# Queries and keys of an attention pass's first head computed in the preceding pass, and unread matmuls around the second layer norm

## The reference, cut to what matters

```python
x1 = _ln(x) * (1.0 + scale1) + shift1
qkv = (x1 @ qkv_w + qkv_b).reshape(Bc, Tc, 3, H, DH)      # 16 heads of 128
attn = softmax(einsum('bthd,bshd->bhts', q, k) * scale)
attn_out = einsum('bhts,bshd->bthd', attn, v) @ out_w + out_b
x = x + gate1 * attn_out
x2 = _ln(x) * (1.0 + scale2) + shift2
x = x + gate2 * (gelu(x2 @ ffn_w1 + ffn_b1) @ ffn_w2 + ffn_b2)
x = x + _L0_attn_ref(x)                                    # a minimal GRU, two 256x256 gates
x = x + _L0_ffn_ref(_L0_cond2_ref(cond, cond, x, ...))     # 32 steps of RK4, then top 4 of 16 blocks
```

## Time and profile before

| | us |
|---|---|
| median of 3 runs | 516.11 |
| the profiled execution | 515.61 |
| its span, from the first to the last instruction | 513.8 |
| PE busy | 449.6 (88%) |
| DVE busy | 434.9 (85%) |
| ACT busy | 316.3 (62%) |
| POOL busy | 48.6 (9%) |

### The profile page before, as it was taken

One profiled execution on the slowest core, in us unless ns is written; L12 is line 12 of the kernel. 1 busy time (PEld: TensorE's weight loads), 2 busy tenths in 40 slices (PEclk: granted clock), 3 DMA queues, 4 the chain that ended last, 5 costly groups with the idle time before them and its releaser, 6 DMA issues.

```text
span 513.8 us, 13730 instructions
## 1 busy us (share of the span) xinstructions
PE 449.6 (88%) x4980; PEld 307.5 (60%) x4980; DVE 434.9 (85%) x1705; ACT 316.3 (62%) x880; POOL 48.6 (9%) x77
## 2 busy tenths in 40 slices
PE   2999989998999899997498997689888888888887
PEld 2655665567556665575244443667676766766666
DVE  4969786787777876889988786999999999999994
ACT  1387855786487748786458755465655646555563
POOL 3010330224021211123000000000000000000000
PEclk9999999999999999999789999698989999999999
DMA  8972402200202000000000000000000000000000
GB/s 294 417 311 63 106 7 76 61 21 0 82 21 62 0 0 1 0 1 0 0 1 1 0 1 0 3 3 0 1 1 11 11 1 10 1 11 11 1 10 22
DMA packets 10127, 20.82 MB, mean 41 GB/s; under 512 B 1456, under 2 KB 4720, under 8 KB 9456
## 3 DMA queue, kind: packets, MB, share of 16 engines
q1 hardware_dynamic: 9536, 19.89, 11.2%
q10 hardware_dynamic: 560, 0.60, 0.3%
HBM read 19.40 MB, written 1.08 MB: 40 GB/s over the span
## 4 chain that ended last, share of the span: by engine, by line
DVE 42%; PE 40%; ACT 6%; issue 5%; POOL 4%; DMA 1%; ACTq 0%; DVEq 0%
PE bank L804 34%; DVE base L1649 5%; DVE lin L1751 5%; POOL ptx L477 4%; DVE qs L1655 4%; DVE cub L1643 3%; PE score L804 3%; DVE sq L1637 3%; DVE pacc L1761 3%; PE spare L804 2%; ACT ao_sb L541 2%; DVE thlo L1633 1%; DMA vec<-vecs 1%; DVE qn L1655 1%; DVE acc L1421 1%
## 5 line engine op out<-in xcount | busy, mean ns | idle before, releaser
L804 PE MATMUL bank<-x,pairs_store 128*128 128x512 f16 x384 | 85.6, 379 | 0.0
L804 PE MATMUL score<-th,coup_part 128*128 128x32 f16 x1024 | 47.2, 179 | 18.1 <-ACT th L788 17.2
L804 PEld LDWEIGHTS bank<-x,pairs_store 128*128 128x128 f16 x384 | 37.1, 98 | 42.8 <-DVE x L1219 0.4
L477 POOL TENSOR_TENSOR ptx<-pt,ptx 32x256 f16<-32x256 f32 x64 | 44.7, 699 | 189.4 <-ACT ptx L573 185.8
L541 ACT ACTIVATE big<-bank,pass_b 128x512 f16<-128x512 f32 x64 | 42.1, 684 | 24.3 <-DVE pass_b L1347 14.4
L788 ACT ACTIVATE th<-qs 128x64 f16<-128x64 f32 x96 | 24.5, 255 | 47.5 <-DVE qs L1655 47.5
L804 PEld LDWEIGHTS score<-th,coup_part 128*128 128x128 f16 x1024 | 34.7, 97 | 31.1 <-ACT th L788 29.7
L1359 DVE SCALAR_TENSOR_TENSOR big<-bank,pass_b,big 128x512 f16<-128x512 f32 x64 | 45.7, 742 | 8.0 <-ACT big L541 7.3
L804 PE MATMUL bank<-pairs_store,ao_sb 128*128 128x256 f16 x384 | 46.6, 273 | 4.7 <-DVE acc L1421 1.4
L804 PEld LDWEIGHTS bank<-pairs_store,ao_sb 128*128 128x128 f16 x384 | 35.5, 97 | 13.6 <-issue 3.6
L804 PE MATMUL bank<-pairs_store,x 128*128 128x512 f16 x192 | 43.4, 379 | 0.0
(11 more groups left out here) (210 smaller groups left out, 1041.8 us busy)
## 6 DMA issues: line engine op xcount, KB each, us to landing
wqk_sb<-wqk SPq DMA_DIRECT2D x16, 256.0 KB, 3.0
wv_sb<-wv SPq DMA_DIRECT2D x4, 512.0 KB, 5.6
wo_sb<-wo SPq DMA_DIRECT2D x4, 512.0 KB, 4.2
f_sb<-ffn_w SPq DMA_DIRECT2D x2, 1024.0 KB, 14.2
ao_sb<-xtok SPq DMA_DIRECT2D x4, 256.0 KB, 6.1
big<-ada_w SPq DMA_DIRECT2D x1, 1024.0 KB, 9.7
x_sb<-xT SPq DMA_DIRECT2D x1, 1024.0 KB, 13.3
w_sb<-w1T SPq DMA_DIRECT2D x1, 1024.0 KB, 16.4
```

What stands on the lines that cost most here:

```text
L477: nc.gpsimd.tensor_tensor(ptx[s, 1, :, s], pt[s], ptx[s, 0, :, s], ALU.subtract).then_inc(ptx_ready, 1)
L804: return nc.tensor.matmul(dst, lhsT, rhs, start=start, stop=stop, **kw)
```

## The change

It moves the queries and keys of a pass's first head to the preceding pass. Those of pass 0 are made ahead of the passes. In passes 0 to 2 `project_next(0, 1)` stands on PE ahead of `mix(2)` and `project_next(2, 3)` ahead of the last two out projections; ACT and DVE have their parts of it at matching places, and the next pass's weights are split there too, with the first head's weights ahead of the fourth emptying of `project(3)`. PE's passes are a loop of three and a last one written out. The numbers of the bank uses are dealt anew. In passes 0 to 2 ACT copies all four strips of the last head's scores, and DVE's order behind them is another; in the last pass DVE's order stays as it was, without the first head. ACT's roundings for the later feed-forward layer (`mlp_highs`) in the last pass are spread: four of the first five stand at values that ACT empties, and the fifth behind three emptyings of `project(3)`. DVE's places for their low parts are the same. The biases of all heads are scaled once, not in each pass.

Then 41 matmuls of 512 columns whose results nobody reads are added: 6 between `turn_x2(0)` and `turn_normed(0)`, 15 behind `turn_normed(0)`, 20 behind `last_gates()`.

```diff
-USE_PROJ = [0, 10, 16, 22]
-USE_V = [4, 5, 6, 7, 8, 9, 14, 15]
-USE_PV = [20, 26, 30, 35]
-USE_OUT = [[28, 29, 32, 37], [33, 34, 38, 39]]
+USE_V = [0, 1, 2, 3, 4, 5, 10, 11]
+USE_PROJ = [[26, 27, 38, 39], [6, 7, 8, 9], [12, 13, 14, 15], [18, 19, 20, 21]]
+USE_PV = [16, 22, 28, 33]
+USE_OUT = [[24, 25, 30, 35], [31, 32, 36, 37]]
...
@@ ScalarE, one pass
+                last = i == NQUAD - 1
+                empty_values(0)
+                if last:
+                    mlp_highs(0, 1)
                 empty_values(1)
...
                 copy_scores(2)
                 empty_projs(3, (0, 1, 2))
+                if last:
+                    mlp_highs(4, 5)
+                else:
+                    weights_high(i + 1, 0)
+                empty_projs(3, [3])
                 exps(2)
-                empty_projs(3, [3])
                 empty_pv(1)
-                copy_scores(3, NB4 // 2)
+                copy_scores(3, NB4 // 2 if last else NB4)
                 place_high(2)
                 exps(3)
+                if not last:
+                    empty_next_proj(0, 1)
                 empty_pv(2)
                 place_high(3)
...
@@ TensorE, one pass
+                def project_next(*ks):
+
+                    if last:
+                        return
+                    if ks[0] == 0:
+                        pe.wait_ge(split_ready, i * NSPLIT + NSPLIT + 1)
+                    for k in ks:
+                        projection(USE_PROJ[0][k], 0, k, fill(USE_PROJ[0][k]))
...
                 def scores(j):
                     if j:
                         pe.wait_ge(scores_copied, i * (QUAD * NB4) + NB4 * j)
+                    else:
+                        for use in USE_V[1:5]:
+                            fill(use)
...
-                project(0)
                 values(0, 1)
                 scores(0)
...
                 out_project(0, 1, [0, 1])
+                project_next(0, 1)
                 mix(2)
...
                 out_project(1, 1, [3])
+                project_next(2, 3)
                 out_project(1, 2, [2, 3])
                 out_project(1, 3, [2, 3])
...
@@ TensorE, behind the passes
+            def unread(dst, count):
+
+                for _ in range(count):
+                    mm(dst, scaled_eye[:], ptx[:, 0, 0:G // 2].rearrange("p g n -> p (g n)"), True, True)
+
+            pe.wait_ge(eye_ready, 1)
             turn_x2(0)
+            unread(spare[:], 6)
             turn_normed(0)
+            unread(spare[:], 15)
...
             last_gates()
+            unread(score[:, 1], 20)
...
@@ VectorE, one pass
-                low_projs(0)
                 low_values(0, 1)
...
-                low_projs(3)
+                last = i == NQUAD - 1
+                for k in range(4):
+                    if k == 3 and not last:
+                        low_weights(i + 1, 0)
+                    low_proj(3, k)
                 low_pv(1, [0])
                 normalise(2)
...
+                else:
+                    low_pv(1, [1])
+                    shift(3)
+                    add_heads(0, 0)
+                    add_heads(0, 1)
+                    normalise(3)
+                    low_first_head(0, (i + 1) * QUAD)
+                    low_first_head(1, (i + 1) * QUAD)
+                    low_pv(2)
+                    add_heads(0, 2)
+                    low_weights(i + 1, 1, 2, 3)
                     low_pv(3)
+                    add_heads(0, 3)
+                    add_heads(1, 0)
+                    add_heads(1, 1)
+                    low_first_head(2, (i + 1) * QUAD)
+                    low_first_head(3, (i + 1) * QUAD)
+                    add_heads(1, 2)
+                    add_heads(1, 3)
```

More of the change, by code:

```diff
@@ L360, in bank_of, with count_of @@
             return use % NBANK
-        def count_of(use, start=0):
-            return start * (USES_PER_PASS // NBANK) + use // NBANK + 1
+        def count_of(use, last=False):
+            if use >= AFTER:
+                return use // NBANK + 1
+            missing = last and use > USE_PROJ[0][1] and bank_of(use) in (1, 2)
+            return FIRST_USES[bank_of(use)] - missing + use // NBANK + 1
         NPAR = USES_PER_PASS // NBANK
@@ L532, in _ @@
             act.wait_ge(ptx_cleared, 1)
+            act.wait_ge(bias_ready, 3)
+            for k, use in enumerate(USE_PROJ[0]):
+                h, w = k // 2, k % 2
+                act.wait_ge(full[bank_of(use)], 1)
+                nc.scalar.activation(qk_sb[:, 0, w, 0, h * HALF:(h + 1) * HALF], bank[bank_of(use)][:], ACT.Identity,
+                                     bias=head_b[:, w, 0:1]).then_inc(high_ready, 1)
             for i in range(NQUAD):
                 def high(use, dst, bias=None):
-                    act.wait_ge(full[bank_of(use)], i * NPAR + count_of(use))
+                    act.wait_ge(full[bank_of(use)], i * NPAR + count_of(use, i == NQUAD - 1))
                     src = bank[bank_of(use)][:]
@@ L581, in empty_values @@
                         high(USE_V[g], v_sb[:, g, 0])
[L583 to L595, removed]
+                last = i == NQUAD - 1
+                empty_values(0)
+                if last:
+                    mlp_highs(0, 1)
                 empty_values(1)
+                if last:
+                    mlp_highs(1, 2)
                 copy_scores(0)
@@ L603, in _ @@
                 empty_values(5)
+                if last:
+                    mlp_highs(3, 4)
                 empty_projs(1, (0, 1))
@@ L840, in _, with projection, attention_pass @@
             ada_chunks(spare[:, D:], 3 * KB, 6 * KB).then_inc(ada2_summed, 1)
-            with pe.Fori(0, NQUAD) as i:
+            def projection(use, j, k, dst):
+                h, w = k // 2, k % 2
+                weights = wqk_pair[:, j % 2].rearrange("p c (k w d) -> p c k w d", k=KB, w=2)
+                sum3(dst[:], [(weights[:, :, n, w], x1_pair[:, :, n, h * HALF:(h + 1) * HALF]) for n in range(KB)]
+                     ).then_inc(full[bank_of(use)], 1)
+            pe.wait_ge(split_ready, 1)
+            for k, use in enumerate(USE_PROJ[0]):
+                pe.wait_ge(x1_ready, k // 2 + 1)
+                pe.wait_ge(free[bank_of(use)], 1)
+                projection(use, 0, k, bank[bank_of(use)])
+            def attention_pass(i, last):
                 def fill(use):
-                    pe.wait_ge(free[bank_of(use)], i * NPAR + count_of(use))
+                    pe.wait_ge(free[bank_of(use)], i * NPAR + count_of(use, last))
                     return bank[bank_of(use)]
                 def taken(use):
-                    pe.wait_ge(free[bank_of(use)], i * NPAR + count_of(use) + 1)
+                    pe.wait_ge(free[bank_of(use)], i * NPAR + count_of(use, last) + 1)
                 def project(j):
                     pe.wait_ge(split_ready, i * NSPLIT + SPLIT_ORDER.index(("qk", j)) + 1)
[L854 to L860, removed]
-                                          for k in range(KB)]).then_inc(full[bank_of(use)], 1)
+                    for k, use in enumerate(USE_PROJ[j]):
+                        projection(use, j, k, fill(use))
+                def project_next(*ks):
+                    if last:
+                        return
+                    if ks[0] == 0:
+                        pe.wait_ge(split_ready, i * NSPLIT + NSPLIT + 1)
+                    for k in ks:
+                        projection(USE_PROJ[0][k], 0, k, fill(USE_PROJ[0][k]))
                 def scores(j):
@@ L1485, in _ @@
                     last_heads(2)
-                assert own.n == STEPS and pairs[0] == PAIRS
+                assert own.n == STEPS and pairs[0] == (i + 1) * PAIRS + (0 if last else 4)
             own.n, own.base = start + NQUAD * STEPS, 0
```

100 lines of the change are left out of this document (60 added, 40 removed).

## The result

| | before | changed |
|---|---|---|
| median, us | 515.95 (515.54 to 516.94, 4 runs) | 523.36 (523.03 to 524.36, 4 runs) |
| ratio | | 1.0144, 95% interval 1.0124 to 1.0164 |
| profiled execution, its span | 515.61, 513.8 | 523.03, 521.3 |

The change makes the kernel 1.4% slower, where 515.2 us was forecast. The forecast's range ended at 517.5.

The account below looks back on a forecast made before the run. PE was taken to pace ordinary passes, DVE the neuron loop. Attention 6.0 - 0.15 - 5.25 = 0.6, taken as 0.8, plus 0.1 for unread matmuls gave 0.9 us off 516.11: 515.2 us, range 512.5 to 517.5.

Parts of the forecast that it names:

- Ordinary passes: Passes 0 to 2: next head's projections fill PE's stops near each pass's end; gain 2.0 us each, 6.0 together.
- Rival 3: Ordinary passes gain only about 1.1 us each, as ACT delays POOL and `mix(3)`; 2.1 lost, 518.2 us; chance 0.13.
- Start of pass 0: In pass 0 `scores(0)` waits for four freed banks at its start, not two; 0.15 us lost once.
- First, the fifth rounding: Last pass: DVE waits for ACT's late fifth rounding of the later layer's weights; everything after is 2.4 us later.
- Rival 1: Last pass loses only one of its two waits, the 2.4 being absorbed; gain 3.3, 512.8 us; chance 0.14.
- Second, the banks: Last pass: `mix(2)` waits for bank 4, emptied late by DVE; both waits together make `mix(3)`'s second part 5.25 us later.
- Everything behind is DVE's chain from 240.14 over the layer norm, unchanged: Behind the last pass's `mix(3)`: DVE sets the pace through the layer norm, and the change adds no loss.
- They delay nothing as long as the clock is full: Second layer norm: the 6 and 15 unread matmuls end before the hidden layer; value zero, bounds -1.8 and +2.16 us.
- rival 2: Clock is on the path: hidden layer's 2.16 us come through, 0.4 at the loop; gain 3.4, 512.7 us; chance 0.07.
- the 0.1 for the 20 ahead of the loop: Behind the gates: 20 unread matmuls may keep the clock up for the neuron loop; 0.1 us gained, bounds 0 and 0.5.
- a last pass more than 6.5 us longer: Sign of a wrong forecast: last pass, first values to last projection, less than 4 or more than 6.5 us longer.
- the page's rule for the clock: Loss is throttled time times one minus clock ratio; some 10 us for two half-clock stretches, not used in the sum.

Follow-up runs that it names:

- e1: Changed kernel with ScalarE making the fifth rounding early, right behind the fourth: 518.91 us, ratio 1.0059 to before.
- e2: Changed kernel with only the bank numbering behind the passes turned by three: 517.83 us, ratio 1.0038 to before.
- e4: Changed kernel with banks numbered without a gap in the last pass and behind it, plus the early fifth rounding: 509.98 us, ratio 0.989 to before.
- e5: Changed kernel without its 41 unread matmuls: 520.61 us, ratio 1.009 to before.
- e7: e4 without the 41 unread matmuls: 510.77 us, ratio 0.9889 to before.
- e9: e1 with 28, 20 and 32 unread matmuls of 128 columns in the last pass's three stops: 517.56 us, ratio 1.0025 to before.
- e3: Changed kernel with banks of the last pass and all behind it numbered without a gap: 512.98 us, ratio 0.9945 to before.
- e6: Kernel before, with the 41 unread matmuls added at the same three places: 515.78 us, ratio 0.9995 to before.
- e8: e4 with 12 and 30 unread matmuls in place of 6 and 15: 510.48 us, ratio 0.9884 to before.

## Why the prediction was wrong

The span was forecast 0.9 us shorter and is 7.5 longer. Of these 8.4 us, 4.8 lie behind the passes, 1.8 in the last pass, 0.9 at the start of pass 0, 0.4 in the ordinary passes, 0.2 behind the start of the output layer, and 0.3 are what the forecast added to its layout.

- **Ordinary passes**, 2.0 us each: the mechanism is right, and they gain 1.9. 54.07 us forecast as 54.0; no stop before `mix(2)`. The stop left before the second part of `mix(3)` is 0.92 us and was put at 0.4, while the wait before `out_project(1, 0, [2])` was put at 0.5 and is 0.2; the two nearly cancel, which is luck. `mix(3)` ends at 181.90, which on the time scale of the kernel before (2.74 us later, by the pass's first values) is 184.64, forecast 184.55. Gain 5.65 in the trace for 6.0 forecast. Rival 3 is out.
- **Start of pass 0**, 0.15 lost: 1.03 in the changed kernel's trace, whose first 24 matmuls take 7.03 us with the clock falling on part of them. In e1, e2, e4, e5, e7 and e9 they run at full clock, `scores(0)` then waits 0.40 us for DVE's emptying, and the first values start at 25.7 to 26.2. The slow clock is not a property of the change; how often it comes no run here shows.
- **"First, the fifth rounding"**, 2.4 us: right. DVE waits 4.61 us for `wv_sb` (4 to 5 were forecast), and it costs 2.3 us between e3 and e4. Rival 1 is out.
- **"Second, the banks"**, 2.85 us: the mechanism and the places are right (waits for `ao_sb`, `acc`, `acc`), the size is not, and the failed step is the full clock at which the layout ran on behind the stops ("PE, waiting for bank 0 until 240.7, then does 24 x 0.110"). Up to there the layout holds: on the time scale of the kernel before (4.62 us later, by the last pass's first values) the changed kernel's second half of `mix(2)` starts at 237.56, forecast 237.75. Around and behind it the granted clock is 0.57 and 0.50 (232 to 236 and 236 to 239 us), and the 16 and the 24 matmuls take 1.89 and 4.09 us, where 1.07 and 2.78 are theirs at full clock: 2.1 us more. In e1 the banks cost 5.1: 2.9 of waits, as forecast, and 2.2 of clock (e9), which the sum left out without a reason. The prediction held a last pass more than 6.5 us longer to show it wrong; it is 7.1 longer.
- **"Everything behind is DVE's chain from 240.14 over the layer norm, unchanged"**: this is the step that failed most, by 4.8 us. The banks were followed to the last pass's `mix(3)` and no further. Output projections (1, 2) and (1, 3) moved from banks 3 and 4 to 1 and 2, while what stands behind the passes kept banks 0, 1, then 2. PE waits for banks that DVE frees only in `last_heads(2)` and `last_heads(3)`, and DVE's way to `last_heads(3)` leads over PE's transposes. e2 shows it: one line on the numbering takes all of it back.
- **"They delay nothing as long as the clock is full"**, said of the unread matmuls, with a bound of -1.8: it holds in the kernel before (e6) and with the banks put right (e4, e7, e8). In the changed kernel the clock was at half and the first 6 stood behind a wait for a bank: 2.5 us (e5), part of the 4.8. The hidden layer's 48 matmuls, forecast at 10.5 us, take 12.15. Speeding them up is worth nothing in e6 and between e7 and e4, so rival 2 is out, and the 0.1 for the 20 ahead of the loop is not to be told from nothing: from the output layer to the end before and e6 take 240.6 and 241.0 us.
- On the page's rule for the clock (the Trainium skill, "TensorE: Matmul & The Clock Gate", section "Terms"): it would give 5 us in the second layer norm before, where a mean of 0.63 over 14 us is 10.4 us at half clock, an estimate by that rule. e6 brings the clock to full there and gains 0.05%, within its interval of zero. In the last pass of e1, where PE is the engine waited for, the clock did cost 2.2 us. The trace disagrees with the rule where another engine holds the path. Where PE does, it bears out the direction: by the rule, 0.66 over 10 us would be 3.4 us in e1, an estimate, and 2.2 were measured.

The range failed because its slow side ended at a last pass that goes as computed. The two large misses have two causes. The waits that a table of banks brings were priced where the diff moved code, and not where the table was merely kept; and those that were priced were priced as waits alone, with the clock at full behind them.

## What to carry to other kernels

When a rotation of buffers is renumbered, follow each buffer past the end of the changed code to its next user, and look at which engine frees it and what that engine waits for in turn; a collision behind the loop cost 4.8 us here and one line removed it. Price a stop of TensorE as the stop and what the clock does behind it, if the matmuls behind it are on the path. Matmuls that hold the clock are free only as long as they stand in TensorE's idle time, and are worth something only where TensorE is waited for.

## What the runs showed of the hardware

- In e1 three stops of 1.75, 1.38 and 2.00 us, with 8 and 16 short matmuls between them, ended with the granted clock at 0.50 (from 232 to 236 us), and 24 matmuls of 256 columns took 5.03 us where they take 2.78. With 80 matmuls of 128 columns in the stops the clock stayed at 1.00 and the same 24 took 2.78.
- Shorter stops at the same place left it at full: 0.44, 0.65, 0.32 and 0.72 us in e4, clock 1.00 from 225 to 236 us.
- The same code met the clock at either level from one execution to the next. The first projections of pass 0 took 7.03 us in the profiles of the changed kernel, e3 and e8, twice about 2.75 with a stop between in e1, e2, e4, e5, e6, e7 and e9, and 5.47 in the kernel before. Behind the stop of 1.93 us for DVE in the last pass, `scores(3)` ran at full clock in the changed kernel and e3, and took 2.63 and 2.70 us in e2 and e5.
